# The scan stage's sum of sixteen matrix powers, from traces, one product and a quotient

## The reference

```
Wx = x @ W.T                            # batch norm folded in; B = 64 images
def step(yt, wx_t):                     # one step for each of the 3136 tokens
    yt = sigmoid(wx_t + yt @ V.T)
    return yt, yt
...
forget_gate = sigmoid(x_ri @ Wf + bf + 2.0)        # fg_r, fg_i: halves of 64 channels
input_gate = sigmoid(x_ri @ Wi + bi)
delta = softplus(x_ri @ Wd + bd) * 0.1
inp_r = delta_r * input_gate_r * Bx_r              # Bx: complex product with B's spectrum
inp_i = delta_i * input_gate_i * Bx_i
def step(h, _):                                    # T = 16 times, h starts at zero
    h_r, h_i = h
    Ah_r = Ar * h_r - Ai * h_i
    Ah_i = Ar * h_i + Ai * h_r
    return (fg_r * Ah_r + inp_r, fg_i * Ah_i + inp_i)
```

## Time and profile before

| | us |
|---|---|
| time, median of 3 runs | 14604.2 |
| lowest and highest of the 3 | 14583.66, 14649.89 |
| profiled execution, its time | 14537.58 |
| its span | 14535.8 |
| PE busy | 11419.5 (79%) |
| DVE busy | 11053.6 (76%) |
| ACT busy | 9833.3 (68%) |
| POOL busy | 4012.8 (28%) |
| TensorE clock granted, mean | 0.81 of full speed |

### The profile page before, as it was taken

One profiled execution on the slowest core, in us unless ns is written; L12 is line 12 of the kernel. 1 busy time (PEld: TensorE's weight loads), 2 busy tenths in 40 slices (PEclk: granted clock), 3 DMA queues, 4 the chain that ended last, 5 costly groups with the idle time before them and its releaser, 6 DMA issues. The chain is left out here.

```text
span 14535.8 us, 248087 instructions
## 1 busy us (share of the span) xinstructions
PE 11419.5 (79%) x87538; PEld 8744.4 (60%) x87538; DVE 11053.6 (76%) x22880; ACT 9833.3 (68%) x22679; POOL 4012.8 (28%) x3975
## 2 busy tenths in 40 slices
PE   7888888888888867777777777777777547776998
PEld 5666666666666645555555555555555235555888
DVE  6777777777777718999999999999999965554133
ACT  6888888888888846666666666667666567776100
POOL 5444444445444421212111211112121111211000
PEclk9999999999999967777777777777777677777555
DMA  3333333333333321111111111111111133333599
GB/s 69 86 81 82 81 82 87 76 90 73 90 77 86 75 61 41 53 53 53 51 47 52 53 53 53 51 46 53 53 52 40 23 84 94 99 90 89 172 316 309
DMA packets 1967708, 1189.72 MB, mean 82 GB/s; under 512 B 48853, under 2 KB 1900056, under 8 KB 1958436
## 3 DMA queue, kind: packets, MB, share of 16 engines
q1 hardware_dynamic: 1554148, 967.87, 26.3%
q10 hardware_dynamic: 408832, 205.55, 5.0%
q0 software_dynamic: 3648, 2.20, 0.1%
HBM read 708.85 MB, written 466.62 MB: 81 GB/s over the span
## 5 line engine op out<-in xcount | busy, mean ns | idle before, releaser
L1236 PEld LDWEIGHTS s_pW<-s_XU,s_vh 128*128 128x128 f32 x6272 | 1415.7, 261 | 1969.1 <-ACT s_XU L1107 1699.7
L1236 PE MATMUL s_pW<-s_XU,s_vh 128*128 128x64 f32 x6272 | 1493.2, 331 | 1071.4 <-ACT s_XU L1107 1071.4
L1107 ACT ACTIVATE s_XU<-s_pW,s_zb 128x64 f32<-128x64 f32 x3136 | 995.7, 318 | 1788.7 <-PE s_pW L1236 1738.1
L1265 PE MATMUL s_pG<-s_wg,s_XNT 128*128 128x384 f32 (+1 forms) x3200 | 1506.0, 559 | 37.5 <-ACT s_Z L1086 37.5
L832 POOL TENSOR_TENSOR s_rst<-s_var,s_epst 128x16 f32<-128x16 f32 (+1 forms) x100 | 141.7, 1417 | 3906.6 <-DVE s_var L79 3906.6
L408 ACT ACTIVATE KB<-pV,qkb 32x392 f32<-32x392 f32 x2048 | 1190.5, 581 | 25.0 <-PE pV L498 1.1
L248 POOL TENSOR_TENSOR SS<-SS,mx 128x784 f32<-128x784 f32 x512 | 769.5, 1503 | 804.8 <-DVE mx L341 804.6
L1203 PEld LDWEIGHTS s_pY<-s_hident,s_XU 128*128 128x128 f32 (+1 forms) x3200 | 752.2, 305 | 177.7 <-issue 129.6
L1711 PE MATMUL c_pS<-c_OX,c_Wm 64*112 64x128 f32 x3584 | 737.6, 420 | 91.1 <-DVE c_X L1727 76.6
L460 ACT ACTIVATE XH<-XR,nm,rs 112x128 f32<-112x128 f32 x1792 | 733.6, 485 | 92.1 <-POOL nm L267 83.6
L506 PE MATMUL pS<-KB,QT 128*64 128x196 f32 x8192 | 793.7, 336 | 0.0
(11 more groups left out here) (249 smaller groups left out, 31958.3 us busy)
## 6 DMA issues: line engine op xcount, KB each, us to landing
XL<-in_x_dram SPq DMA_DIRECT2D x64, 1568.0 KB, 12.4
XR<-in_x_dram SPq DMA_DIRECT2D x64, 1568.0 KB, 18.0
x_dram<-XR SPq DMA_DIRECT2D x64, 1568.0 KB, 8.1
xh_dram<-XH SPq DMA_DIRECT2D x64, 1568.0 KB, 8.1
r_X<-x_dram SPq DMA_DIRECT2D x64, 1568.0 KB, 14.2
c_X<-x_dram SPq DMA_DIRECT2D x64, 1568.0 KB, 19.4
out_dram<-c_X ACTq DMA_DIRECT2D x64, 1568.0 KB, 13.9
s_XQ<-xh_dram ACTq DMA_DIRECT2D x384, 256.0 KB, 2.8
```

What stands on the lines that cost most here:

```text
L1107: act.activation(XU[j % 2][:, t, :], pW[t // R % 2][:, B * (t % R):B * (t % R) + B], ACT.Tanh, bias=zb[:, 0:1], scale=0.5).then_inc(u_sb, 1)
L1236: pe.matmul(pW[t // R % 2][:, B * (t % R):B * (t % R) + B], vh[:], before, start=False, stop=True, skip_group_check=True).then_inc(z_ps, 1)
L1265: pe.matmul(pG[i % 3][0:tc, 0:3 * C], XNT[:, i, 0:tc], wg[:], start=True, stop=True).then_inc(g_ps, 1)
```

## The change

The sum is no longer multiplied out as four factors (1 + M)(1 + M^2)(1 + M^4)(1 + M^8), row by row of the matrix. The traces of M, M^2, M^4, M^8 and M^16 are multiplied instead, and the sum becomes two coefficients, one for `Wv` and one for `IN`, with a division by det(1 - M). The division is Exp(-Ln(...)) on ACT. On DVE, four full operations and seven half operations of a group become eleven half operations, and one half operation comes in before L993; on ACT, seven squares become seven squares, a Ln and an Exp.

```
-    NV = 24
-    NA = 7
+    NV = 25
+    NA = 9
...
                     did(dve.scalar_tensor_tensor(d0, tf[:, 0], 1.0, d0, ALU.add, ALU.mult))
+                    after(4)
+                    did(dve.tensor_tensor(f0[:, 0], d0, t0, ALU.subtract))
                     dve.wait_ge(sp_d, o * 2 + 2)
...
                     dve.wait_ge(am, o * NA + 5)
-                    did(dve.scalar_tensor_tensor(t2, d1, 2.0, t2, ALU.mult, ALU.subtract))
-                    if conv:
-                        dve.wait_ge(n_ps, oc * NQ + NQ)
-                    did(dve.scalar_tensor_tensor(f1[:, 1], t1, -1.0, d1, ALU.add, ALU.mult))
-                    did(dve.scalar_tensor_tensor(f0[:, 0], f0[:, 0], -0.25, d0, ALU.add, ALU.add))
-                    did(dve.scalar_tensor_tensor(t0, t0, 1.0, d0, ALU.add, ALU.mult))
-                    dve.wait_ge(am, o * NA + 6)
-                    did(dve.scalar_tensor_tensor(f1[:, 0], f1[:, 0], -0.25, d1, ALU.add, ALU.subtract))
+                    did(dve.scalar_tensor_tensor(t2, d1, -2.0, t2, ALU.mult, ALU.add))
+                    did(dve.tensor_tensor(t1, t0, t1, ALU.mult))
                     dve.wait_ge(am, o * NA + 7)
-                    did(dve.scalar_tensor_tensor(t1, t1, -0.25, d2, ALU.add, ALU.subtract))
-                    did(dve.scalar_tensor_tensor(t2, t2, -1.0, d2, ALU.add, ALU.mult))
+                    did(dve.scalar_tensor_tensor(f1[:, 0], d2, -2.0, f1[:, 0], ALU.mult, ALU.add))
+                    after(13)
+                    did(dve.tensor_tensor(t2, t2, f1[:, 0], ALU.mult))
+                    after(14)
+                    did(dve.tensor_tensor(t1, t1, t2, ALU.mult))
+                    dve.wait_ge(am, o * NA + 9)
+                    did(dve.scalar_tensor_tensor(f1[:, 1], d1, -2.0, f1[:, 1], ALU.mult, ALU.add))
                     after(15)
-                    did(dve.scalar_tensor_tensor(rows(f1), both(t1), 1.0, rows(f1), ALU.add, ALU.mult))
+                    did(dve.scalar_tensor_tensor(f1[:, 0], t0, -2.0, t1, ALU.add, ALU.mult))
                     after(17)
-                    did(dve.tensor_tensor(rows(f1), rows(f1), both(t2), ALU.add))
+                    did(dve.tensor_tensor(f1[:, 0], f1[:, 0], f1[:, 1], ALU.subtract))
                     after(18)
-                    did(dve.scalar_tensor_tensor(rows(f0), both(f1[:, 0]), 1.0, rows(f0), ALU.add, ALU.mult))
+                    did(dve.scalar_tensor_tensor(f0[:, 0], f1[:, 0], 2.0, f0[:, 0], ALU.add, ALU.mult))
                     after(19)
-                    did(dve.tensor_tensor(rows(f0), rows(f0), both(f1[:, 1]), ALU.add))
+                    did(dve.scalar_tensor_tensor(t0, t0, -1.0, f0[:, 0], ALU.add, ALU.mult))
                     after(20)
-                    did(dve.scalar_tensor_tensor(rows(wv), both(f0[:, 0]), 1.0, rows(wv), ALU.add, ALU.mult))
-                    did(dve.scalar_tensor_tensor(rows(inp), both(f0[:, 1]), 1.0, rows(inp), ALU.add, ALU.mult))
-                    after(22)
+                    did(dve.tensor_tensor(t0, t1, t0, ALU.subtract))
+                    did(dve.tensor_tensor(rows(wv), both(f0[:, 0]), rows(wv), ALU.mult))
+                    after(21)
+                    did(dve.tensor_tensor(rows(inp), both(t0), rows(inp), ALU.mult))
+                    after(23)
...
                     if o is not None and k == 6:
                         needs(4)
                         act.activation(t1, t0, ACT.Square).then_inc(am, 1)
-                        act.activation(f0[:, 0], t0, ACT.Square, bias=cols[0:tm, 1:2]).then_inc(am, 1)
+                        act.activation(d1, d0, ACT.Square).then_inc(am, 1)
                     if o is not None and k == 8:
-                        act.activation(d1, d0, ACT.Square).then_inc(am, 1)
-                    if o is not None and k == 14:
+                        needs(5)
+                        act.activation(f0[:, 0], f0[:, 0], ACT.Ln, bias=cols[0:tm, 3:4], scale=2.0).then_inc(am, 1)
                         act.wait_ge(am, o * NA + 3)
-                        act.activation(d2, d1, ACT.Square).then_inc(am, 1)
+                        act.activation(f0[:, 0], f0[:, 0], ACT.Exp, scale=-1.0).then_inc(am, 1)
...
                     if o is not None and k == 16:
-                        needs(8)
+                        needs(9)
                         act.activation(t2, t1, ACT.Square).then_inc(am, 1)
+                        act.activation(d2, d1, ACT.Square).then_inc(am, 1)
                     if o is not None and k == 20:
+                        needs(11)
                         if conv:
                             act.wait_ge(bx_d, oc + 1)
-                        act.activation(f1[:, 0], t1, ACT.Square, bias=cols[0:tm, 2:3]).then_inc(am, 1)
+                        act.activation(f1[:, 0], t2, ACT.Square).then_inc(am, 1)
+                        act.wait_ge(am, o * NA + 6)
+                        act.activation(d1, d2, ACT.Square).then_inc(am, 1)
                     if o is not None and k == 22:
-                        needs(11)
-                        act.wait_ge(am, o * NA + 6)
-                        act.activation(t1, t2, ACT.Square, bias=cols[0:tm, 2:3]).then_inc(am, 1)
+                        needs(13)
+                        act.activation(f1[:, 1], f1[:, 0], ACT.Square).then_inc(am, 1)
```

More of the change, by code:

```diff
@@ L707, in scan_phase @@
         nmr = sb("nmr", [TF, OS])
-        cols = sb("cols", [P, 3])
+        cols = sb("cols", [P, 4])
         pW = [ps(f"pW{i}", [C, 512]) for i in range(2)]
@@ L808, in _ @@
             pool.memset(cols[:, 1:2], 0.5)
-            pool.memset(cols[:, 2:3], -0.5).then_inc(pch, 1)
+            pool.memset(cols[:, 2:3], -0.5)
+            pool.memset(cols[:, 3:4], 2.0).then_inc(pch, 1)
             pool.wait_ge(pch, 1)
@@ L955, in bounded @@
                 dve.wait_ge(pa_d, b0 + 6)
-                dve.scalar_tensor_tensor(pa[:, 4 * HC:5 * HC], s_, -1.0, c_, ALU.mult, ALU.subtract).then_inc(pa_d, 2)
+                dve.scalar_tensor_tensor(pa[:, 4 * HC:5 * HC], s_, 1.0, c_, ALU.mult, ALU.add).then_inc(pa_d, 2)
                 dve.wait_ge(pa_d, b0 + 8)
@@ L991, in _ @@
                     did(dve.scalar_tensor_tensor(d0, tf[:, 0], 1.0, d0, ALU.add, ALU.mult))
+                    after(4)
+                    did(dve.tensor_tensor(f0[:, 0], d0, t0, ALU.subtract))
                     dve.wait_ge(sp_d, o * 2 + 2)
                     did(dve.scalar_tensor_tensor(flat(dl), flat(dl), 88.0, flat(z), ALU.min, ALU.max))
-                    after(5)
+                    after(6)
                     did(dve.scalar_tensor_tensor(flat(dl), flat(ti), 1.0, flat(dl), ALU.add, ALU.mult))
-                    after(6)
+                    after(7)
                     dve.wait_ge(bx_d, o + 1)
@@ L1003, in _ @@
                 if o is not None:
-                    after(7)
+                    after(8)
                     turned_by(tm, Wv, inp, a, wp_d, wv_d, o)
-                    dve.wait_ge(am, o * NA + 3)
-                    did(dve.scalar_tensor_tensor(t1, d0, -2.0, t1, ALU.mult, ALU.subtract))
+                    dve.wait_ge(am, o * NA + 2)
+                    did(dve.scalar_tensor_tensor(t1, d0, -2.0, t1, ALU.mult, ALU.add))
                     dve.wait_ge(wv_d, o + 1)
@@ L1041, in _ @@
+                    after(23)
                     did(dve.scalar_tensor_tensor(flat(wv), flat(wv), 0.5, flat(inp), ALU.add, ALU.add))
-                    after(23)
+                    after(24)
                     did(dve.tensor_tensor(flat(inp).rearrange("t (b r c) -> t b r c", b=OS, r=2),
@@ L1081, in gate @@
                 if i == 0:
-                    wait(act, dv, (oc - 1) * NV + 9)
+                    wait(act, dv, (oc - 1) * NV + 10)
                 bank = pG[i % 3][0:tc]
```

## The result

| | before | after |
|---|---|---|
| time, median, us | 14607.5 (4 runs) | 14895.26 (4 runs) |
| lowest and highest of after | | 14889.64, 14902.58 |
| span of the profiled execution | 14535.8 | 14887.7 |

The ratio is 1.02, with a 95% interval of 1.0184 to 1.0215: the changed kernel is slower. Forecast were 14,863 us and a sum of +259 us; the medians differ by 288. The two profiled spans differ by 352. Of that, 288.5 lie in the scan stage, and the other 64 in the expert stage behind it, which the change does not touch: 2,887 us against 2,824 us, at a mean granted clock of 0.63 against 0.65. The medians agree with the part of the scan stage, so that part is what has to be explained.

The account below looks back on a forecast made before the run. The prediction took the recurrence of PE and ACT as the bound, DVE only in the last chunks. Cycles +269, first slots +14 (together +282) and last groups -23 gave +259 on the median 14604.2: 14,863 us, range 14,770 to 15,000.

Parts of the forecast that it names:

- DVE is not the bound: Scan stage: PE and ACT's recurrence sets the pace until the last chunks; rival that DVE does: 14,327 us, 3%.
- k = 8, +3.86: ACT's step from tanh 8 to tanh 9: two table loads, Ln and Exp make it 5.02 us against 1.16.
- k = 16 hidden: ACT's square added at k = 16 is covered by waits for PE; rival, more exposed work: 14,997 us, 12%.
- k = 20 +0.86: ACT at k = 20: a square comes in and one loses its bias column, +0.86 us a slot, counting in full.
- No new wait of ACT for DVE: ACT's squares at k = 20 and 22 find DVE's results ready, with 1 us in hand.
- Slot s = 0, -1.4: In slot s = 0 ACT's wait for POOL goes and `XN` starts 2.2 us earlier; the slot is 1.4 us shorter.
- Slots s = 1 to 3, +4.54 each: ACT's additions and savings sum to 4.54 us more in each of these three slots of a cycle.
- the cycle, 12.2 us: The cycle of four slots becomes 12.2 us longer, in 22 cycles.
- TensorE's clock: Rival: PE's granted clock rises two steps later, 1.8 us in each of 91 slots, 160 us: 15,025 us, 8%.
- mean granted clock "would fall": Part of the rival on PE's clock: its mean granted clock of 0.75 would fall.
- The last chunks, -23: In the last nine groups DVE is the bound and saves 2.8 us each, less small waits: -23 us.
- The first three slots, +14: Three slots of the first chunk with a group, outside the 22 cycles, add 14 us.

Follow-up runs that it names:

- e2: From the kernel before: the four full DVE operations L1030 to L1036 work on half their columns, so the sum is wrong; 14519.04 us, ratio 0.9965.
- e5_square_at_14: From the changed kernel: ACT's square `d2` moves back from k = 16 to k = 14; 14904.96 us, ratio 1.0208 to the kernel before.
- e8_square_at_24: From the changed kernel: ACT's square `d1` of k = 20 goes to k = 24 (22 in s = 3); 14805.62 us, ratio 1.0138 to the kernel before.
- e3_reciprocal_on_dve: From the changed kernel: DVE's reciprocal ahead of `BX` replaces ACT's Ln and Exp; 15064.14 us, ratio 1.034 to the kernel before.
- e7: From the kernel before: the square of `t0` into `t1` goes from k = 6 to k = 2 in slots s = 1 to 3; 14580.07 us, ratio 0.9991.
- e9: From the kernel before: square of `t0` at k = 2 in slots s = 1 to 3, DVE's L1022 and L1023 ahead of `BX`; 14563.79 us, ratio 0.998.
- e10: From the kernel before: only DVE's L1022 and L1023 moved ahead of `BX`; 14579.71 us, ratio 0.9993.
- e11: From the kernel before: e9 plus the square of L1129 at k = 3 in slots s = 1 and 2; 14566.11 us, ratio 0.9977.
- e4: From the kernel before: ACT's square of k = 8 becomes load, Ln, load, Exp, DVE's work unchanged, sum wrong; 14876.12 us, ratio 1.0211.
- e6: From the changed kernel: Ln goes to k = 24 and Exp to k = 26 in slots s = 1 and 2; 14823.19 us, ratio 1.015 to the kernel before.
- e12_both_and_shorter: From the kernel before: e11 and e2 together, so the sum is wrong; 14498.66 us, ratio 0.9928.
- e1_no_table_loads: From the changed kernel: Ln and Exp of k = 8 become two squares, so the coefficients are wrong; 14699.61 us, ratio 1.01 to the kernel before.

## Why the prediction was right, and where it was off

*DVE is not the bound*: shown. The cycle grew although DVE had 2.8 us less a group, and did not fall with e2's 4.3 less. Where DVE does touch the recurrence, in s = 0, being earlier did let `XN` start earlier, in the change and in e2. The Trainium skill ("Perfetto Trace Analysis", section Identifying the Most-Contended Engine) would have had the busiest engine made faster; e2_shorter_dve did that, and its cycle stayed at 249.2.

*k = 8, +3.86*: measured +3.89 (5.05 against 1.16). Ln and Exp cost what squares of their size do (1.15 and 1.06, taken as 1.14 and 1.05). The Trainium skill's drain of 1380 ns ("ScalarE: Activation LUTs", section What ACT_TABLE_LOAD costs) stands in none of the switches here: 1.31 us from one operation to the next, with the load.

*k = 16 hidden, k = 20 +0.86*: both shown, by e5_square_at_14 (no change) and by e8_square_at_24 (steps 20 to 24 from 5.80 to 4.86).

*No new wait of ACT for DVE*: the cover of 1 us held in the change and was used up in e3_reciprocal_on_dve.

*Slot s = 0, -1.4*: -1.0 (76.5 to 75.5). The wait is gone. `XN` came 2.7 earlier behind the softplus, not 2.2, since ACT reached it 3.2 us later than before and not 3.77: the steps of k = 0 and k = 5 were 0.25 shorter each, with recurrence matmuls of 0.44 in place of 0.69. The steps 16 to 20 took 1.0 back (6.83 in place of 5.83).

*Slots s = 1 to 3, +4.54 each*: +4.5, +5.6 and +4.5. Two of the three are within 0.1. The one that is not, s = 2, has the late rise: 6.87 for steps 16 to 20 in place of 5.75.

*The term that was mis-sized is the cycle, 12.2 us*: it grew by 13.8, or 303 in place of 269 over 22 cycles. The rival "TensorE's clock" named the cause, but took it as all or nothing, 1.8 us in each of 91 slots. The runs show 1.0 and 1.1 us in two slots of four, s = 0 and s = 2, which, less the 0.5 us that s = 0 gained at k = 0 and k = 5, make up the difference of about 1.5. That the mean granted clock "would fall" was also wrong: over the 22 cycles it is 0.75 in both kernels, so a late rise cannot be read from the mean.

*The last chunks, -23*: -27.5. *The first three slots, +14*: +13.2.

What stands shown beyond this is that the sum of the terms is not the cycle. The kernels fall on few lengths: 249.2 in before, e2, e7, e9, e10 and e11; 262.8 in after, e4 and e5; 259.4 in e6 and e8; and e3 stands by itself at 269.65. In each group kernels with different amounts of work in the recurrence end at the same length, as the rise moves between 3.0 and 6.35 us and with it up to 1.5 us a slot. In e2 and e7 the account closes: the four slots of a cycle are 3.8 and 3.6 us shorter up to k = 16, and their steps 16 to 20 are 3.9 and 3.6 us longer. So the 4.54 a slot were right as a count of ACT's work, and that their sum came out within 1.6 of the cycle was partly luck: e2 with -2.2 in the same count gave 0, and e8 with -2.8 gave -3.4. Only e12_both_and_shorter and e1_no_table_loads, where slots of one kind differed from cycle to cycle, lie between.

What stays open is what decides on the moment of the rise, and why the cycle falls on these lengths. No run held the clock still, so that the clock takes the savings back is read from where the microseconds went, in every slot, and not from an experiment on the clock itself. The 0.2% of e9 and e11 is not placed. The case in which both loops get shorter without anything left out stands untested, since the edit of e10 did not shorten DVE's.

## What to carry to other kernels

A busy engine that waits for another in every period need not be the bound; count the work that stands in the chain of the recurrence, switches of activation tables first: two of them cost 2.6 us a slot here, in a place where 2.8 us less on VectorE could not pay for them. Moving work of such an engine into one of its waits gains nothing if it then waits as long for the next input (e10). In a periodic loop in which TensorE's granted clock falls and rises, compare the position of the rise and the length of the period before and after every edit: in two kernels savings of 3.6 and 3.8 us a period were given back there in full, and in a third one of 2.8 us made the period 3.4 shorter. The sum of the steps saved does not tell which of the two it will be. Where an operation has to go into such a chain, put it where the other engine has work of its own (k = 24 and not k = 8 or k = 20).

## What the runs showed of the hardware that was not expected

- The granted clock of TensorE rose from 1.2 to 2.4 GHz 3.0 us behind the first gate matmul in one slot and 5.9 behind it in the next, with the same instructions in the same order. Kernels of different work kept the period while this interval moved: the middle one of the 22 cycles is 249.2 us long in six kernels and 262.8 in three, to 0.02 us.
- DVE's RECIPROCAL of 128x1024 f32 takes 6.55 us, where a scalar_tensor_tensor of the same size takes 1.22 and the tensor_scalar before it 0.69.
- A switch of activation tables between two dependent ACTIVATEs costs 1.31 us, all of it but 0.03 the load, and no third load stands between the Exp and the tanh behind it (7897.88 to 7898.84).
